# Row of the bias fold fetched for 128 partitions, and a denser order of routing steps, in a two-layer gated kernel

## What is computed

```python
x = x + top2_of_8_experts(ln(x), gate_input=ctx)         # A: relu MLP, hidden 512, expert biases
x = x + grouped_top4_of_16_experts(ln(x))                # B: silu(x W1+b1) * (x W3+b3), W2, b2
x = x + cross_attention(ln(x), ctx, ctx)                 # C: 16 heads of width 8
x = x + 0.5 * (silu(ln(x) @ fc1 + b) @ fc2 + b)          # D
```

## Time and profile before

| | us |
|---|---|
| median of three runs | 886.69 |
| the profiled execution | 887.16 |
| its span, first to last instruction | 884.2 |
| TensorE busy | 763.7 (86%) |
| VectorE busy | 633.5 (72%) |
| ScalarE busy | 502.1 (57%) |
| GpSimd busy | 398.2 (45%) |

### The profile page before, as it was taken

The page is one execution under the profiler, slowest core; times in us unless marked ns, Lnnn a source line. Parts: engine busy times, 40 slices in busy tenths (PEclk is TensorE's granted clock), DMA queues, the critical chain, the costliest instruction groups (busy, mean ns, idle before and its releaser), DMA issues.

```text
span 884.2 us, 17572 instructions
## 1 busy us (share of the span) xinstructions
PE 763.7 (86%) x5374; PEld 584.3 (66%) x5374; DVE 633.5 (72%) x1875; ACT 502.1 (57%) x990; POOL 398.2 (45%) x462
## 2 busy tenths in 40 slices
PE   7489787786998889798879999978999998997897
PEld 5478676675887678687668888844555554554675
DVE  6878533453856958666976788677888887885786
ACT  2755433453775466577546677724565555555796
POOL 5447773006710077751037774046766444455100
PEclk9689977987999999989999999989999999999899
DMA  9294556465411222911213432034455446441011
GB/s 325 89 336 147 187 175 205 166 194 172 125 59 48 79 71 65 359 52 27 68 48 90 124 85 56 24 106 120 134 144 145 119 117 177 110 125 49 13 37 48
DMA packets 96368, 106.54 MB, mean 120 GB/s; under 512 B 12604, under 2 KB 70348, under 8 KB 94999
## 3 DMA queue, kind: packets, MB, share of 16 engines
q1 hardware_dynamic: 76856, 78.04, 28.2%
q0 software_dynamic: 8608, 18.22, 8.1%
q10 hardware_dynamic: 10816, 9.16, 3.4%
HBM read 69.19 MB, written 36.18 MB: 119 GB/s over the span
## 4 chain that ended last, share of the span: by engine, by line
PE 52%; DVE 19%; POOL 9%; issue 8%; ACT 4%; ACTq 3%; DMA 3%; SPq 2%; DVEq 0%; POOLq 0%
PE y_ps L1937 4%; PE y_ps L2067 3%; ACTq L1650 3%; PE y_ps L2166 3%; PE hid_ps L2052 3%; POOL yg L657 2%; POOL xr L648 2%; PE hid_ps L2142 2%; PE hid_ps L2154 2%; PE hid_ps L1925 2%; PE hid_ps L2143 2%; PE tr_ps L2222 2%; DVE hl L1147 2%; PE hid_ps L2036 2%; PE y_ps L1939 1%
## 5 line engine op out<-in xcount | busy, mean ns | idle before, releaser
L648 POOL DMA_INDIRECT xr<-b_tokens,idx_sb x70 | 67.5, 964 | 121.8 <-DVE idx_sb L909 100.6
L1147 DVE TENSOR_TENSOR hl<-hid_ps,hh 128x512 fp32r<-128x512 f32 x78 | 53.7, 689 | 87.0 <-ACT hh L1577 86.5
L657 POOL DMA_INDIRECT yg<-a_rows,idx_a x64 | 61.2, 957 | 79.5 <-DMA a_rows<-yo 56.2
L1937 PE MATMUL y_ps<-region,hh 128*128 x312 | 88.3, 360 | 8.9 <-DVE hl L1147 8.4
L1334 DVE TENSOR_REDUCE negmax<-hid_ps 128x4 f32<-128x512 f32 x128 | 85.8, 683 | 7.3 <-PE hid_ps L2143 6.9
L679 POOL DMA_INDIRECT yg<-b_rows,idx_b x64 | 62.3, 973 | 37.9 <-issue 35.5
L1571 ACT ACTIVATE zb<-hid_ps 128x512 f32<-128x512 f32 x78 | 46.5, 596 | 53.9 <-PE hid_ps L1917 42.9
L2143 PE MATMUL hid_ps<-region 128*128 128x512 f32 x128 | 75.9, 594 | 0.0
L2067 PE MATMUL y_ps<-region,hh 128*128 x280 | 74.8, 344 | 0.1
L1937 PEld LDWEIGHTS y_ps<-region,hh 128*128 128x128 f32 x312 | 62.5, 200 | 16.8 <-issue 16.3
L1925 PE MATMUL hid_ps<-ident,zb 128*128 128x128 f32 x312 | 51.7, 292 | 25.1 <-ACT zb L1571 25.1
(11 more groups left out here) (359 smaller groups left out, 2302.6 us busy)
## 6 DMA issues: line engine op xcount, KB each, us to landing
region<-k_strips SPq DMA_DIRECT2D x128, 64.0 KB
region<-k_strips SPq DMA_DIRECT2D x32, 256.0 KB, 3.0
region<-hl SPq DMA_DIRECT2D x128, 64.0 KB
k_strips<-k_halves SPq DMA_DIRECT2D x24, 256.0 KB, 4.3
region<-nought SPq DMA_DIRECT2D x6, 1024.0 KB
a_rows<-yo SPq DMA_DIRECT2D x20, 256.0 KB
b_rows<-yo SPq DMA_DIRECT2D x18, 256.0 KB
staged<-a_w_in SPq DMA_DIRECT2D x16, 256.0 KB, 5.7
```

The costliest lines, as they stand in the source:

```text
L648: g.indirect_dma_start(xr[:, q % 3, j * RB:j * RB + w], None, src, bass.IndirectOffsetOnAxis(ap=rows.bitcast(U32), axis=0)).then_inc(x_til ...
L657: g.indirect_dma_start(yg[:, b % 2, k, j * P:(j + 1) * P], None, ys[h], bass.IndirectOffsetOnAxis(ap=idx[:, h, k, t:t + 1].bitcast(U32), a ...
L1147: v.tensor_tensor(hl[:, n % 2, :], hid_ps[2 + n % 2][:], hh[:, n % 2, :].bitcast(F32), ALU.subtract).then_inc(a_hl, 1)
L1937: t.matmul(y[:, c0:c0 + 2 * P], hh[:, n % 2, cs], w2a[:, bass.ds(e * (2 * FA) + c * 2 * P, 2 * P)], start=c == 0, stop=False)
```

## The change

Three edits. The row of the fold goes to all 128 partitions of its buffer (the function is renamed, VectorE still uses 127 of them). The table of steps for the first half is changed: `best_b`/`top_b` from T = 28/29 to 25/26, `prefix` from 25 to 26, `tile_bases`/`slots_b` from 26/27 to 27/28, `weights_b` 30 to 29, the hots 31 to 33 to 30 to 32, `inverse` 33/34 to 32/33, `tile_experts` 34 to 33, `inverted` 35 to 33. The second half's entries are the same.

```diff
         SGM, GRP, MSK, PRE, TOP, POS, WTS, HOT, EID, INV, SLT = (
-            (23, 20), (24, 22), (25, 23), (25, 24), (28, 23), (26, 25), (30, 27), (31, 28), (34, 31), (33, 30), (35, 31))
+            (23, 20), (24, 22), (25, 23), (26, 24), (25, 23), (27, 25), (29, 27), (30, 28), (33, 31), (32, 30), (33, 31))
...
-        def last_row(k):
-            return rt[0:P - 1, raw_slot(k) * BT:(raw_slot(k) + 1) * BT]
+        def row_copies(k):
+            return rt[:, raw_slot(k) * BT:(raw_slot(k) + 1) * BT]
...
-                        v.tensor_tensor(rows, rows, last_row(k), ALU.subtract).then_inc(b_folded, 1)
+                        v.tensor_tensor(rows, rows, row_copies(k)[0:P - 1], ALU.subtract).then_inc(b_folded, 1)
...
-                        a.dma_start(last_row(k), bass.AP(row.tensor, row.offset, [[0, P - 1], [1, BT]])).then_inc(in_raw[raw_slot(k)], 16)
+                        a.dma_start(row_copies(k), bass.AP(row.tensor, row.offset, [[0, P], [1, BT]])).then_inc(in_raw[raw_slot(k)], 16)
```

## The result

The changed kernel takes 843.78 us (median of 4 runs, 839.75 to 844.09) against 888.71 us in the same comparison (886.65 to 892.41): a ratio of 0.947, 95% interval 0.943 to 0.951, so 5.3% faster. The forecast was 843 us, range 834 to 860. The profiled execution took 839.75 us and is the shortest of the four; its span is 838.0 us against 884.2.

What follows compares the result with a forecast made beforehand. It took stage A to be held by ScalarE's long DMA issues behind a one-engine row fetch, and the list of slots to come late for GpSimd. 887.16 - 40 (row fetch) - 4 (steps) = 843.2 us, predicted 843, range 834 to 860.

Steps and rivals of the forecast that it cites:

- The row fetch: Stage A: 128 partitions spread over 16 engines end ScalarE's long issues; 39.5 us by stalls, 42.5 by pace, 41 taken.
- (a): Second half's slots load after GpSimd's last scatter: there at 150 us, needed at 153; 1.3 us late if it takes 9.1.
- (b): DMA traffic of stage A's 28 steps pressed into 77 us: 282 GB/s, under the 360 GB/s carried elsewhere.
- (c): GpSimd's gathers of A's first half, asked for in steps 45 and 48: second block up to 2 us late; 1 us off.
- The denser steps: Routing part of stage A: list of slots 4.4 us sooner, at 302.9 us; stage A's end only about 1 us sooner.
- Who gains: GpSimd's chain from the list to block 6's gathers, started earlier: 4 us gained, ends 0 and 6 us.
- the wait of 3.64 us for block 6: VectorE's wait for gathered rows at 368.94 us: 3.4 us of it taken away; sign of success: gone or under 1 us.
- the low end: Gain of GpSimd's earlier start is 0 if the clears of stage C's buffers, from 353 us on, hold the landing.
- Rival 1: Stage A's hidden waits (scatters, gathers, stores) eat 10 to 20 us of the gain: 853 to 863 us; chance 0.20.
- Rival 2: The row fetch is not spread, because one source row serves all partitions; only the steps gain: 883 us; chance 0.06.
- Rival 3: 16 engines reading the same 2 KB hinder each other, each fetch holding all for 10 to 13 us: 897 to 910 us; chance 0.03.
- Rival 4: Transfers land so much sooner that other waits shrink too, 6 to 10 us more: 832 to 836 us; chance 0.07.

Runs made afterwards that it cites:

- rows127_distinct: The kernel before, with the fetch over 127 partitions reading 127 different rows of W2 instead of one row 127 times: 888.73 us in a single execution.
- rows125: The kernel before, with the one row fetched into 125 partitions and subtracted from 125 rows: 849.89 us in a single execution.
- rows_only: The kernel before with only the row fetch over 128 partitions, old table of routing steps: 849.11 us, ratio 0.958 to the kernel before.
- steps_only: The kernel before with only the new table of routing steps, row fetch still over 127 partitions: 882.70 us, ratio 0.995.
- clears_late: The changed kernel with the clears of stage C's buffers three groups later: 1039.12 us on the third chip, beside 1034.80 for the changed kernel.

## Why the prediction was right, and where it wasn't

The total is right to 1 us, and the two mechanisms (one engine for 127 partitions, GpSimd's chain started earlier) are the ones that the forecast named. That it is as close as 1 us is luck: the stalls were worth 1.6 us more than the 41 supposed, what is next late 4.6 us more than the 1 supposed, and the table some 1 us more than 4. Step by step:

**The row fetch.** That 127 partitions go through one engine, and that the long issues come with that and not with the single source row, is shown by `rows127_distinct` and `rows125`. Why an issue behind a slow fetch is held, no run shows. The forecast rested on 128 partitions being spread over 16 engines, and no row of the trace before shows that; the changed kernel shows a fetch at a share of 0.58 and 184 GB/s (94.6 to 95.1 us; the 360 GB/s of the estimate were not reached in it), landings in 3.4 to 6.2 us and no issue above 0.352 us. Of the two ways to size it, the pace was exact: 42.5 us forecast, 42.6 us measured by row 46, 2.75 us a step as supposed. The sum of the stalls, 39.5 us, was too low, and the clock (0.83 before, 1.00 after) fits the reason given for it.

**What is next late (a): GpSimd's scatters and the slots load.** SyncE now waits 6.8 us for the last scatter, issues the first of these loads at 147.43 us, and it lands 3.3 us later, at 150.7. TensorE comes to it at 152.74 us without a wait (one of 0.4 us for a group gathered earlier is in the trace). The forecast had 150 and 153 us; with a load of 9.1 us its own numbers give 1 us late and not 1.3. Right, with 2 us to spare.

**(b): DMA traffic.** 282 GB/s forecast, 271 measured, at a share of 0.85. It was not a bound in stage A's own steps. The landings in (c) are longer than supposed; whether the traffic does it, no run shows.

**(c): the gathers of A's results.** Here the term was mis-sized. I took off 1 us; 5.6 us went between rows 46 and 58, and the row fetch alone gave 38.5 us, not 40. The gathered rows were not later than I put them: GpSimd starts 3.4 us after row 39 and not 5.8, the landing takes 5.5 and 4.7 us (183.24 to 187.95) instead of 3, and the two blocks are there 17.8 and 27.0 us after row 39 (160.94 us), where the forecast had 19 and 29. But VectorE asks sooner: rows 39 to 46 take 16.2 us (160.94 to 177.17), 2.3 us a step, and not 19.3. The pace of 2.75 us is a mean over steps of unlike length, and I used it for seven of them; that gives the two waits of 0.9 us. And I left out a third user of the same queue: the root behind the third block, which is the largest of the three waits, 2.1 us. The clock that falls behind it was left out too. I counted the gathers in GpSimd's queue and not the small instruction that stands behind them.

**The denser steps.** The list of slots was to come 4.4 us sooner; against row 64 of line 1147 (270.16 and 232.74 us) it comes (307.31 and 265.54 us) 37.1 us after it at first and 32.8 us after the change, 4.3 us. (From `rows_only` to `steps_only`, the same difference of tables, it is 38.1 and 33.5 us, 4.6 us.) The end of stage A was to be 1 us sooner and is 1.2 us sooner (309.75 - 270.16 = 39.6 us against 271.15 - 232.74 = 38.4 us). TensorE's wait for `inverse`, priced at nothing, brought nothing to the list: `inverted` follows `row_index` at once. All right.

**Who gains.** I took 4 us, and `steps_only` measured 4.9 us. But one sign that I named failed: the wait of 3.64 us for block 6 was to fall under 1 us and is 3.68 us. The chain says why the gain came all the same. The last gather of that block is issued at 321.20 us, 41.9 us sooner than before, and VectorE is released at 328.08 us, 40.9 us sooner; the landing has got 1 us longer (6.9 us from the issue instead of 5.9), with the DMA engines at a share of 0.96 and 363 GB/s in the changed kernel too (314 to 330 us).

VectorE itself came earlier by as much. From the last row of line 1147 to its release at block 6 it takes 59.2 us before and 56.9 us after, since two other waits for GpSimd, which stood there before, are gone (timeline of the kernel before):

```profile
334.31 0.88 DVE L1031 SCALAR_TENSOR_TENSOR X<-yg,gates,X 128x128 f32<-128x128 f32 x3 [0.90 <-DMA yg<-a_rows,idx_a]
...
365.14 0.16 DVE L980 SCALAR_TENSOR_TENSOR nbias<-mvs,rstds 128x4 f32<-128x4 f32 x1 [1.01 <-POOL rstds L611]
```

`rows_only` has both too (0.69 and 1.01 us), `steps_only` and the changed kernel have neither, so they go with the table. I had steps only 1 us sooner up to block 6, and looked at its wait alone. So that wait stayed, and both sides of it moved: the mechanism was right (GpSimd's earlier start pays), the place where it pays was not. The size holds: `steps_only` is 1.9 us behind the kernel before at row 64 of line 1147 and 2.0 us ahead from row 15 of line 1280 to the end of stage B, so the table gives 3.9 us there. (From `rows_only` to the changed kernel it is 6.8 us between the same rows; each is one execution.) That the clears hold this landing was forecast as the low end; `clears_late` was to show it and could not.

**After stage B.** I let all behind 369 us move as a block. From row 35 of line 1280 (466.2 and 422.9 us, 43.3 us apart) to the end the distance grows to 46.2 us in the profiled executions, while the medians are 44.9 us apart. The changed kernel's other three runs are 4 us above the profiled one, so I read nothing into it. `steps_only` gains another 3.3 us and `rows_only` 0.9 us on the kernel before behind stage B, where no edit reaches; why is open.

**Rivals.** Rival 1 (gain eaten in stage A) was right in kind with 5.6 us, far under its 10 to 20. Rival 2 falls with the result itself (one source row for 128 partitions, and no long issue) and with `rows127_distinct`. Rival 3 falls with the landings: 3.4 to 6.2 us, and no issue above 0.352 us. Rival 4 didn't show.

## What to carry to other kernels

A transfer over 127 partitions ran on one DMA engine here (a share of 0.07 of 16 engines, 26 GB/s) and held the issuing engine's whole program at its next DMA by up to 10.02 us, while 125 and 128 partitions did not. Look for long issues of a DMA on a compute engine's queue, look at the transfer ahead of them, and try 128 partitions even if some are not used. The gain of the removed stalls was sized better by the pace of like steps beside them (42.5 us for 42.6) than by the length of the stalls (39.5 us); but a mean pace over 28 steps does not say when a single step comes (2.3 instead of 2.75 us here). And when steps get faster, walk each other engine's queue from its first wait to its last instruction, the small ones behind the large ones too.

## What was not expected of the hardware

An issue of a DMA by ScalarE lasted up to 10.02 us, though the DMA that it issued was an ordinary one of 128 rows; the one ahead of it in the same queue was the slow one. The six long issues all end 10.1 to 14.1 us after the issue of the fetch ahead of them. Not every issue behind a slow fetch was held: the one at 189.53 us took 0.33 us, 8.7 us after its fetch, and the one at 88.66 us took 0.36 us, 5.5 us after the first fetch of all (83.12 us), while the next, also 5.5 us after its fetch, took 7.83 us. So the distance in time does not decide it; what does is open. And the same kernel took 844 us on one chip and 1035 us on another, with 178 us of ScalarE's standing still unexplained by any record.
